# Moving the units of the maximum pass in TensorE's order: two places per step instead of three, and a stream that begins at 0.09 of a group

## What is computed

```python
q, k, v = (heads(x @ W.T + b) for W, b in ((Wq, bq), (Wk, bk), (Wv, bv)))
sim = einsum('bhid,bhjd->bhij', q, k) + bias * SCALE      # bias = rel_emb[bucket(i - j)]
sim = sim + where(j > i, -inf, 0)
out = einsum('bhij,bhjd->bhid', softmax(sim), v)
x = x + out @ Wo.T + bo
```

## Time and profile before

| what | us |
|---|---|
| median of 3 runs | 401.53 |
| lowest and highest | 400.35, 402.07 |
| the profiled execution | 402.29 |
| span of its profile | 400.5 |
| PE busy in the span | 321.0 |
| DVE busy | 287.5 |
| ACT busy | 184.0 |

### The profile page before, as it was taken

The page is one execution under the profiler, slowest core; times in us unless marked ns, Lnnn a source line. Parts: engine busy times, 40 slices in busy tenths (PEclk is TensorE's granted clock), DMA queues, the critical chain, the costliest instruction groups (busy, mean ns, idle before and its releaser), DMA issues.

```text
span 400.5 us, 8158 instructions
## 1 busy us (share of the span) xinstructions
PE 321.0 (80%) x3197; PEld 153.1 (38%) x3197; DVE 287.5 (72%) x960; ACT 184.0 (46%) x258; POOL 69.5 (17%) x78
## 2 busy tenths in 40 slices
PE   0182438396999899799889979988988998999982
PEld 0131215143334335334434433443443344337752
DVE  3985356358668589588678848967875996773986
ACT  1042024131655554575565545556555545873330
POOL 9812035700001000100100100010010000161552
PEclk9996586668699999999999989999998999999998
DMA  8013422410012101201201220331222010100011
GB/s 227 26 53 116 145 90 95 148 64 3 2 43 66 39 18 52 81 1 61 75 12 44 68 64 2 86 88 26 65 79 55 15 16 12 33 2 10 5 52 53
DMA packets 18295, 21.97 MB, mean 55 GB/s; under 512 B 5584, under 2 KB 14960, under 8 KB 18256
## 3 DMA queue, kind: packets, MB, share of 16 engines
q1 hardware_dynamic: 18256, 21.45, 18.5%
HBM read 14.98 MB, written 4.23 MB: 48 GB/s over the span
## 4 chain that ended last, share of the span: by engine, by line
PE 51%; DVE 17%; DMA 15%; ACT 7%; issue 5%; SPq 4%; POOL 1%; DVEq 0%; POOLq 0%; ACTq 0%
PE ps L1015 14%; PE ps L1044 13%; PE ps L1001 13%; DMA QA<-mrow 7%; ACT PT L626 6%; PE ps L1032 5%; DMA qk_scratch<-QS 4%; DVE FM L759 3%; DVE XN L701 2%; DVE junk L766 2%; DMA KA<-qk_scratch 2%; DMA rows<-in_vectors 2%; PE ps L1077 2%; DVE st L836 1%; DVE U L889 1%
## 5 line engine op out<-in xcount | busy, mean ns | idle before, releaser
L626 ACT ACTIVATE PT<-ps 128x1024 f32<-128x1024 f32 (+1 forms) x192 | 145.8, 810 | 132.4 <-PE ps L1032 101.9
L759 DVE TENSOR_REDUCE FM<-ps 128x1 f32<-128x512 f32 (+3 forms) x176 | 108.4, 660 | 29.2 <-PE ps L1001 29.1
L1001 PE MATMUL ps<-KA,QA 96*128 96x256 bf16 (+3 forms) x544 | 108.7, 294 | 17.6 <-DMA KA<-qk_scratch 14.3
L1015 PE MATMUL ps<-QA,KA 98*128 98x512 bf16 (+3 forms) x384 | 99.0, 343 | 25.4 <-DMA QA<-mrow 10.3
L766 DVE CUSTOM_DVE_ANT_0 junk<-ps,NB 128x256 bf16<-128x256 f32 (+1 forms) x224 | 78.8, 403 | 37.3 <-PE ps L1001 37.2
L1044 PE MATMUL ps<-PT,VG 128*16 128x512 f32 (+3 forms) x768 | 86.9, 498 | 0.0
L1001 PEld LDWEIGHTS ps<-KA,QA 96*128 96x128 bf16 x544 | 44.1, 101 | 103.7 <-DVE FM L759 32.9
L1015 PEld LDWEIGHTS ps<-QA,KA 98*128 98x128 bf16 x384 | 32.5, 101 | 52.5 <-ACT PT L626 21.6
L497 POOL COPY NB<-NBH 128x1024 bf16<-128x1024 bf16 x7 | 7.3, 1040 | 212.3 <-PE ps L1044 211.4
L1032 PE MATMUL ps<-TT,flb 128*32 128x176 f16 (+4 forms) x1152 | 38.9, 245 | 0.0
L1032 PEld LDWEIGHTS ps<-TT,flb 128*32 128x32 bf16 x1152 | 21.5, 96 | 17.9 <-issue 17.0
(11 more groups left out here) (88 smaller groups left out, 255.5 us busy)
## 6 DMA issues: line engine op xcount, KB each, us to landing
QA<-qk_scratch SPq DMA_DIRECT2D x48, 96.0 KB
KA<-qk_scratch SPq DMA_DIRECT2D x16, 288.0 KB
TT<-f_scratch SPq DMA_DIRECT2D x16, 120.0 KB, 7.8
qk_scratch<-QS SPq DMA_DIRECT2D x4, 384.0 KB
qk_scratch<-QS SPq DMA_DIRECT2D x12, 128.0 KB
X<-in_x SPq DMA_DIRECT2D x2, 512.0 KB, 6.2
out<-U SPq DMA_DIRECT2D x4, 256.0 KB, 2.3
xnT<-OT SPq DMA_DIRECT2D x28, 32.0 KB
```

The source lines that it names most:

```text
L626: nc.scalar.activation(PT[:, s % 3, 2 * q:2 * q + 2, off:off + w], ST[:, q, :, off:off + w], ACT.Exp).then_inc(s_exp, 1)
L759: nc.vector.tensor_reduce(FM[:, ib, heads[0]:heads[-1] + 1, piece], bank[:, 0:w * len(heads)].rearrange("p (h n) -> p h n", n=w), AX.X, AL ...
L1001: last = nc.tensor.matmul(bank[:, i * w + j - j0:i * w + j - j0 + n], QA[0:KS, p, ib // 4, h, (ib % 4) * 128:(ib % 4 + 1) * 128], KA[0:KS, ...
L1015: last = nc.tensor.matmul(ST[:, q, h % 2, off:off + w], KA[0:KST, p, jb // 4, h, (jb % 4) * 128:(jb % 4 + 1) * 128], QA[0:KST, p, ic, h, o ...
```

## The change

The constants move the stream's beginning and end earlier, m1 with them, and `places()` gives place 1 no share of the time, so that no unit of a steady group falls there. In the loop, what place 1 holds now stands before the second half of the scores.

```diff
-        half = 2 * step_cols(ic, jb)[1] + (640 if near_cols(ic, jb) else 0)
-        for pos, cost in enumerate((half, half, 4.2 * step_cols(*STEPS[s])[1])):
+        half = 2 * step_cols(ic, jb)[1]
+        rest = 4.2 * step_cols(*STEPS[s])[1] + (1200 if near_cols(ic, jb) else 450)
+        for pos, cost in enumerate((half + rest / 2, 0, half + rest / 2)):
...
-S_START, S_END, M1_AT = 0.15, 1.03, 1.06
+S_START, S_END, M1_AT = 0.09, 0.965, 1.0
...
                     s_units_at(s, 0)
+                    s_units_at(s, 1)
                     if at:
                         scores(*at, 1)
-                    s_units_at(s, 1)
-                    if at:
                         biases(*at[1:])
```

## The result

| | us |
|---|---|
| changed kernel, median of 4 runs | 413.06 (411.63 to 417.02) |
| kernel before, median of 4 runs | 401.8 (400.35 to 403.81) |
| ratio, 95% interval | 1.0324 (1.0256 to 1.0392) |
| span of the profile, changed, before | 412.0, 400.5 |
| change forecast, measured | +8.5, +11.3 (+11.5 in the profiles) |

The change makes the kernel slower by 3.2%. The direction was forecast, the size was not: 1.0324 times 401.5 is 414.5, just above the range. Single runs of one kernel differ by several us, the longest with a lower mean clock (in the first experiment 401.46 us at 0.93 of the full clock, 415.4 us at 0.90), so a ratio here is over the runs within 1.5% of their kernel's fastest, while a median is over all of them.

The account below looks back on a forecast made before the run. PE bounds step 4's scores to step 11's biases, SP's load the rest. 8.5 + 0.2 + 0.3 - 0.2 + 0.2 + 0.9 = 9.9, less 0.9 is 9; 401.5 + 9 = 410.5, said 410 us, range 399 to 414.

Parts of the forecast that it names:

- Part 1: Load's issue to step 4's scores: m1 issued some 2 us earlier still waits for the load's tail, 0 us.
- Part 2: One unit moves from the load-bound stretch into the PE-bound one, 30 units instead of 29: +0.2 us a group.
- Part 3: Step 4's scores to step 11's biases: bunched units wait for banks DVE frees, +1.5 us a group, bounds 1.2 to 1.8.
- the walk: Unit-by-unit timing of PE, DVE and three banks from step 4's scores: waits sum to 1.8 us a group.
- Group 0: First group: only order within places changes much; one more unit ahead of step 11's biases, +0.2 us.
- The gathers: Three groups where a gather follows m1's DMAs, now starting 2 us earlier into the load's tail: +0.2 us in all.
- Group 6: Group with four reciprocals on DVE, taken as already paced by DVE: +0.3 us.
- Behind group 6: After the last biases of that group no load follows, so the exchanged unit gives 0.2 us back.
- The clock: Longer waits for m1's rows cause one more clock fall, +0.9 us; 0.9 taken off because falls and bunches hide each other.
- The rival with four more falls: Clock falls behind every longer wait for m1's rows: 5.2 us instead of 0.9, 414 us; chance 0.1.
- The wait: Rival: m1's earlier packets pass the load's tail, six waits ahead of step 4's scores go, 396 us (389 without bunches); chance 0.15.
- The banks: Rival: DVE's spare 3.4 us of 21.2 absorbs the bunches, leaving the exchanged unit and perhaps a fall, 403 us; chance 0.2.

Follow-up runs that it names:

- the first experiment: Kernel before with only the three constants changed (0.09, 0.965, 1.0), places and loop order as before: 0.9974, median 408.98 us.
- the load spread: Load of KA's 72 rows issued as three DMAs of 24 rows instead of one: kernel before 381.47 us (0.9402), changed kernel 389.75 us (0.9622).
- the filled pair: Changed kernel and kernel before, each with six needless matmuls ahead of PE's wait for m1's rows in groups 1 to 6: 409.85 and 400.88 us.
- the plain one: Changed kernel and kernel before, both without the six needless matmuls: 413.06 and 401.8 us.

## Why the prediction was right or wrong

**What bounds the kernel: right.** PE in the one part of a group and the load in the other describe every profile with the load in one DMA: the distances sum to 73.6 to 74.7 us in seven of them, and to 76.3 in the one with m1's DMAs from ACT. With the load spread, PE's own work and its waits for ACT make most of the distance.

**Part 1, m1 earlier, 0 us: right in size, its reason half right.** The six distances sum to 73.7 us before and 73.8 after. m1's packets do wait for the load's tail; that they stand behind it in SP's order is not needed for it, as ACT's queue showed. With the load spread, the tail, the wait and the falls of the clock went together.

**Part 2, the exchanged unit: right**, 0.2 of the 0.5 us that remained with a shorter reduction on DVE.

**Part 3, the bunches, 1.5 us: right to 0.2.** With part 2 it made 1.7; 1.5 was measured in each of the groups 1 to 5 of the filled pair, and in the groups 1 and 3 of the plain one, where the clock stayed full; the second scores behind m0 came within 0.1 us of the walk, and shortening DVE's work took 1.0 of it away. What is left for the bunches is 1.3, between the bounds 1.2 and 1.8 and near the lower; that the old small delays vanish in the new waits fits this and was not tested apart. That PE would wait ahead of m0 above all, the profile does not show as idle time: nearly all the waits for DVE that it lists are at the units (line 1002).

**Group 0, 0.2 us: not seen.** Its stretch took 25.39 us instead of 25.49, in part at the lower clock in both. **The gathers, 0.2 us: not seen,** with the six distances equal to 0.1.

**Group 6, 0.3 us: wrong by 1.3.** The prediction held it for paced by DVE already, since its stretch was 23.1 us. Of that 1.3 us was a fall of the clock; the spread load shows 21.72 us for the old order at a full clock (282.32 to 304.04 above), and the new one takes 23.34. The order costs 1.6 us here too, hidden in the comparison by a fall that the changed kernel did not have at this place.

**Behind group 6, -0.2: wrong by 0.7.** From the last biases of group 6 to the end it took 72.0 us before and 71.0 after. No units of a next group follow there, so not one unit but three left it (33 to 35).

**The clock, 0.9 us, less 0.9 for overlap: the term that failed.** The forecast priced more falls at nothing in the end; they cost 3.0 us. The changed kernel's profile has 13.6 us at half clock in the groups (3.41 us each from 172.8 and from 282.0, 6.82 us from 244.5), that of before 6.8 us. In the groups 1 to 5 this added 4.3 us, and in group 6 it gave 1.3 back: 3.0 us. The deduction for hiding was not real: a stretch in which both meet, 24.24 us, is the sum of both, 22.76 and 1.5. The rival with four more falls (414) was nearer in time than the forecast, and partly by luck: the time at half clock doubled, but behind three of the six waits the clock stayed full. How often it falls differs from run to run, and what decides it is open.

The sum as measured in the profiles: 7.5 for groups 1 to 5, 1.6 and -0.9 for group 6 and what follows, 3.0 for the clock, 0.3 ahead of the first load, 11.5 us. The order itself is 8.2 of it, against 8.8 forecast (8.5 for groups 1 to 5, 0.2 for group 0, 0.3 for group 6, less 0.2 at the end); its errors are -1.0 in the groups 1 to 5, -0.2 in group 0, 1.3 in group 6 and -0.7 behind it. What carried the time out of the range is the clock: without its 3.0 us the profiles differ by 8.5, the +8.5 of the forecast, though in part because errors of the order cancel.

**The rivals.** The wait did not go. The banks did not carry the bunches; that they carried group 6's reciprocals, which come evenly, was no evidence for bunches, as the prediction itself held against it.

## What to carry to other kernels

When two engines exchange work through a few buffers, an order is to be judged by walking each buffer's release, not by the busy shares: DVE had 3.4 us to spare in 21, and PE still lost 1.3 to bunches. An earlier issue helps only if the issue sets the landing; compare the same small DMA with and without traffic ahead first. And where a large transfer moves at a rate that is a few engines' share of sixteen, split it before reordering anything around it: here that was worth 6%, nearly half of it ahead of the groups 1 to 6, and the change under study aimed at the symptom.

## What the runs showed of the hardware

Behind PE's waits for m1's rows the clock stayed at its full level in some groups and fell to half in others: it stayed behind 1.12, 1.73 and 1.78 us in the changed kernel, and fell behind 1.79, 2.15 and 2.63. In the kernel before it fell behind 1.72 us, and with the shorter reductions it fell behind 1.84 us twice and stayed behind 2.11, 2.22 and 2.23:

```profile
169.67 0.61 PE L1021 MATMUL ps<-QA,KA 98*128 98x512 bf16 x1 [1.84 <-DMA QA<-mrow]
169.67:173.08 3.41, 3.41 (x17) 1.29 (x18) 0.69 (x1) 2.09 (x3) 0.00 (x0) 0.50 0.00 0
...
242.50 0.61 PE L1021 MATMUL ps<-QA,KA 98*128 98x512 bf16 x2 [2.22 <-DMA QA<-mrow]
242.50:245.90 3.40, 3.40 (x28) 1.52 (x32) 2.10 (x4) 2.75 (x4) 0.00 (x0) 1.00 0.01 4
```

So the length of a wait alone did not tell whether the clock would fall. A kernel with such waits has a time that scatters: the ten runs of the constants alone took 401.46 to 415.4 us, and the profile, of the longest of them, has 27 us at half clock in the groups (four times 6.83 us); the four runs of the kernel before with the spread load, where these waits were gone, took 377.82 to 382.71 us.

A second queue did not carry a small DMA past a large load: six packets of 1 KB from ACT's queue moved only with the load's last packets, 1.8 to 2.6 us behind the two that passed, while 121 packets of SP's queue went through. Why is left open; it was not tried with two large transfers.
